# A graph network on one NeuronCore: the last scaling of the output moves from VectorE and ScalarE to GpSimd

## The reference, cut to what matters

```python
def _layernorm(x, axis=-1, eps=1e-5):
    m = jnp.mean(x, axis=axis, keepdims=True)
    v = jnp.var(x, axis=axis, keepdims=True)
    return (x - m) / jnp.sqrt(v + eps)

# layer 0: two gated steps (m = adj @ (x @ W), gates by sigmoid and tanh), each with a relu
x = _layernorm(x + _L0_gnn_ref(x, adj, ...))
# layer 1: each row weighs its last 100 neighbours by powers of 1/2
support = input @ weight
mask = (adj != 0)
rank = jnp.cumsum(mask, axis=1); deg = rank[:, -1:]
k = jnp.minimum(deg, 100.0); pos = rank - (deg - k)
w = mask * jnp.where(pos > 0, 0.5 ** (k - pos), 0.0)
x = _layernorm(x + w @ support + bias)          # this layernorm's division is what the change moves
```

## Time and profile before

| what | value |
|---|---|
| median of 3 executions | 377.87 us (377.56 to 378.74) |
| the profiled execution | 378.1 us, of it the span of the profile 376.4 us |
| TensorE busy | 350.5 us (93%) |
| VectorE busy | 301.3 us (80%) |
| ScalarE busy | 152.6 us (41%) |
| GpSimd busy | 25.6 us (7%), 16 powers of it 23.7 us |
| last stores | 8 of 128 KB, 1.9 us from issue to landing |

### The profile page before, as it was taken

The page is one execution under the profiler, slowest core; times in us unless marked ns, Lnnn a source line. Parts: engine busy times, 40 slices in busy tenths (PEclk is TensorE's granted clock), DMA queues, the critical chain, the costliest instruction groups (busy, mean ns, idle before and its releaser), DMA issues.

```text
span 376.4 us, 6453 instructions
## 1 busy us (share of the span) xinstructions
PE 350.5 (93%) x2424; PEld 161.3 (43%) x2424; DVE 301.3 (80%) x476; ACT 152.6 (41%) x185; POOL 25.6 (7%) x32
## 2 busy tenths in 40 slices
PE   4896979999999999999999889999999999979993
PEld 1331324243333333333332224353544453869992
DVE  1488979797876968889966597969897999888993
ACT  0003303022031210312113246848677868676992
POOL 1000000000000000000000020202020201102242
PEclk9999999999999999999999999999999999998999
DMA  7999999999999999998999999999999996100011
GB/s 231 404 393 392 409 381 407 376 410 362 407 405 351 386 300 407 376 367 341 343 348 321 398 377 352 341 339 336 356 346 369 379 374 237 30 0 4 2 57 57
DMA packets 36366, 117.38 MB, mean 312 GB/s; under 512 B 4208, under 2 KB 8560, under 8 KB 36336
## 3 DMA queue, kind: packets, MB, share of 16 engines
q1 hardware_dynamic: 36336, 116.97, 83.9%
HBM read 114.86 MB, written 1.05 MB: 308 GB/s over the span
## 4 chain that ended last, share of the span: by engine, by line
PE 71%; DMA 15%; ACT 5%; DVE 4%; issue 2%; POOL 1%; SPq 1%; POOLq 0%; DVEq 0%; ACTq 0%
PE m_acc L433 40%; DMA stream<-in_adj_t 12%; PE out L433 12%; PE out L533 6%; PE rz_ps L491 4%; PE n_ps L491 3%; PE rz_ps L506 3%; DMA hx<-in_x_pairs 2%; ACT codes L684 2%; PE m_acc L465 1%; ACT s_mid L684 1%; POOL rstd L775 1%; ACT stream L684 1%; PE out L475 1%; DVE codes L1015 1%
## 5 line engine op out<-in xcount | busy, mean ns | idle before, releaser
L433 PE MATMUL m_acc<-stream,s_in 128*64 128x512 f32 x512 | 126.7, 606 | 7.3 <-DMA stream<-in_adj_t 7.1
L834 DVE TENSOR_SCALAR codes<-stream 128x1024 uint8<-128x1024 f32 x128 | 83.8, 686 | 14.6 <-DMA stream<-in_adj_t 14.4
L433 PE MATMUL m_acc<-stream,s_mid 128*64 128x512 f32 x280 | 67.6, 604 | 1.7 <-DMA stream<-in_adj_t 1.7
L433 PEld LDWEIGHTS m_acc<-stream,s_in 128*64 128x64 f32 x512 | 34.0, 137 | 72.8 <-issue 44.6
L433 PE MATMUL out<-stream,s_mid 128*64 128x512 f32 x232 | 58.6, 594 | 0.3 <-DMA stream<-in_adj_t 0.2
L775 POOL TENSOR_TENSOR rstd<-var,mhalf 128x4 f32<-128x4 f32 x16 | 23.7, 1486 | 347.1 <-DVE var L983 347.1
L880 DVE SCALAR_TENSOR_TENSOR codes<-codes,run 128x1024 uint32<-128x1024 uint32 (+2 forms) x36 | 39.8, 1106 | 1.2
L875 DVE TENSOR_TENSOR run<-run,codes 128x2048 uint16<-128x2048 uint16 (+2 forms) x35 | 38.4, 1098 | 1.2
L684 ACT ACTIVATE wexp<-codes,code_bias 128x2048 uint16<-128x2048 uint8 x18 | 35.7, 1990 | 2.1 <-PE out L533 2.1
L684 ACT ACTIVATE codes<-codes,code_bias 128x2048 uint16<-128x2048 uint8 x16 | 31.6, 1987 | 0.0
L615 ACT ACTIVATE m_high<-m_acc 64x512 f32<-64x512 f32 x14 | 8.3, 594 | 57.2 <-PE m_acc L433 46.9
(11 more groups left out here) (143 smaller groups left out, 354.2 us busy)
## 6 DMA issues: line engine op xcount, KB each, us to landing
stream<-in_adj_t SPq DMA_DIRECT2D x212, 512.0 KB, 6.2
hx<-in_x_pairs SPq DMA_DIRECT2D x8, 128.0 KB, 8.4
mx<-in_x_t SPq DMA_DIRECT2D x8, 128.0 KB, 6.4
mx<-hx SPq DMA_DIRECT2D x16, 64.0 KB, 4.9
x_res<-in_x_pairs SPq DMA_DIRECT2D x8, 128.0 KB, 5.8
out_nodes<-stream SPq DMA_DIRECT2D x8, 128.0 KB, 1.9
const<-in_consts SPq DMA_DIRECT2D x1, 358.0 KB, 7.9
bias_b<-in_bias SPq DMA_DIRECT2D x1, 128.0 KB, 8.1
```

The source lines that it names most:

```text
L433: last = nc.tensor.matmul(to[D * u:D * (u + 1), :], state[:, t * D:(t + 1) * D], stream[:, n % SLOTS, u * CW:(u + 1) * CW], start=start[u] ...
L834: nc.vector.tensor_scalar(edges(p // 2, b, 2 * (p % 2), 2), stream[:, n % SLOTS, :], 0.0, None, ALU.not_equal).then_inc(mask_made, 1)
```

## The change

GpSimd scales all eight output chunks, each right behind its power, with one multiplication of 128x256 (`y` by `rstd`, both f32 in SBUF). It waits for its own power and for `y`. VectorE and ScalarE scale none: VectorE's loop loses five instructions and its tenth turn, ScalarE's loses twelve. SyncE waits for one semaphore instead of two.

```diff
-OUT_ACT = (0, 2, 4)
...
             for i in range(NCH):
-                if i in OUT_ACT:
-                    sp.wait_ge(o_by_act, OUT_ACT.index(i) + 1)
-                else:
-                    sp.wait_ge(o_by_dve, i + 1 - sum(a < i for a in OUT_ACT))
+                sp.wait_ge(out_scaled, i + 1)
                 sp.dma_start(out[NCH - 1 - i], o_n[:, i]).then_inc(out_stored, 16)
...
                 expand_next(ACT_END[i])
-                if i - 2 in OUT_ACT:
-                    b = i - 2
-                    act.wait_ge(rstd_made, NCH + b + 1)
-                    for k in range(KT):
-                        last = nc.scalar.activation(o_n[:, b, k, :], y[:, b, k, :],
-                                                    ACT.Copy, scale=rstd[:, b, k:k + 1])
-                    last.then_inc(o_by_act, 1)
...
             for i in range(NCH):
                 to_rstd(NCH + i, i)
+                pool.wait_ge(rstd_made, NCH + i + 1)
+                pool.wait_ge(y_made, i + 1)
+                nc.gpsimd.tensor_tensor(o_n[:, i], y[:, i],
+                                        rstd[:, i, :].unsqueeze(2).to_broadcast([P, KT, D]),
+                                        ALU.mult).then_inc(out_scaled, 1)
...
-            def scale_out(i):
-                dve.wait_ge(rstd_made, NCH + i + 1)
-                nc.vector.tensor_tensor(o_n[:, i], y[:, i],
-                                        rstd[:, i, :].unsqueeze(2).to_broadcast([P, KT, D]),
-                                        ALU.mult).then_inc(o_by_dve, 1)
...
-            for i in range(NCH + 2):
+            for i in range(NCH + 1):
...
-                if i >= 2 and i - 2 not in OUT_ACT:
-                    scale_out(i - 2)
```

More of the change, by code:

```diff
@@ L342, in build @@
         half_made, y_made = sem("half_made"), sem("y_made")
-        o_by_act, o_by_dve = sem("o_by_act"), sem("o_by_dve")
+        out_scaled = sem("out_scaled")
         out_stored = sem("out_stored")
```

## The result

| kernel | median | range | executions |
|---|---|---|---|
| before | 377.71 us | 376.77 to 384.1 | 20 |
| changed | 379.55 us | 377.74 to 518.4 | 20 |

A forecast was written before the change was run, and what follows sets the result against it. TensorE bounds the whole span; in the last 25 us TensorE, VectorE and ScalarE are in balance. The end's +1.16 and TensorE's +0.85 make +2.0 on the median of 377.87: 379.9 us, range 378.0 to 381.9.

The forecast's parts named there:

- X: Price of one 128x256 multiplication on GpSimd, taken as 0.65 us from the element-wise set-up instructions.
- rival B: A GpSimd multiplication costs 1.0 us or more, a power's fixed part being any TENSOR_TENSOR's; +1.1 unblocked, +4.1 blocked; chance 0.15.
- C: Rival: GpSimd pays some microsecond for each change between power and multiplication; over 381 us; chance 0.03.
- GpSimd's wait for its own instruction, 0.2: A GpSimd instruction that waits for the one before it starts 0.2 us behind its end.
- The end, +1.16: Behind TensorE's last share, two powers and two multiplications stand in one line on GpSimd; the end moves by +1.16 us.
- "Add eps" blocked: In the output loop "add eps" waits for the port that GpSimd's multiplication holds, 0.58 us late in each of four turns.
- TensorE's end, +0.85: Four slips of 0.58 less 0.68 for scalings gone delay chunk 6's `y` by 1.64; TensorE ends 0.85 us later.
- The sum, +2.0: The end's +1.16 plus TensorE's +0.85 us make the whole change +2.0 us slower.
- Rival A: "Add eps" needs no port or gets it first; TensorE ends 0.79 us earlier, +0.4 in all, 378.2 us; chance 0.31.

The follow-up runs named there:

- experiment 9: The changed kernel with chunk 6's multiplication in two pieces of 128x128 and chunk 7's in four of 128x64; one execution, 379.0 us.
- 1: The changed kernel, but GpSimd scales only chunks 0 to 5 and VectorE 6 and 7; ratio to the kernel before 1.0021, +0.8 us.
- 10: GpSimd scales chunks 0 to 5, VectorE 6 and 7, with "add eps" moved ahead of the expansion; ratio to the kernel before 0.9995, -0.2 us.
- 3: The changed kernel with "add eps" of the output chunks made a reduction over pairs; ratio to the kernel before 1.0008, +0.3 us.
- 6: The kernel before with only "add eps" of the output chunks made a reduction over pairs; ratio to the kernel before 0.9998, -0.1 us.
- 7: GpSimd scales chunks 0 to 5, each in two multiplications of 128x128, VectorE 6 and 7; ratio to the kernel before 0.9979, -0.8 us.
- 5: The kernel before with chunks 0 to 5 stored unscaled, VectorE scaling 6 and 7; ratio to the kernel before 0.9977, -0.9 us.
- 2: GpSimd scales only chunks 6 and 7, ScalarE and VectorE 0 to 5 as before; ratio to the kernel before 1.0033, +1.2 us.
- 4: GpSimd scales chunks 0 to 5, VectorE 6 and 7, with "add eps" of the output chunks a reduction; ratio to the kernel before 0.9971, -1.1 us.
- 8: "Add eps" a reduction, GpSimd scaling 0 to 6, VectorE 7, chunk 6's sum and "add eps" before the last-share wait; ratio to before 0.9977, -0.9 us.

## Why the prediction was right, and where its sizes were off

- **The multiplication, X = 0.65.** Measured 0.61. The guess from element-wise set-up instructions held, down to its parts: 0.19 fixed and 1.7 ns per element for two inputs, both as experiment 9 has them. The power's 1.01 is no fixed price of a TENSOR_TENSOR (one of 128x64 takes 0.29): rival B is out. So is C: a power behind a multiplication still takes 1.01.
- **GpSimd's wait for its own instruction, 0.2.** Measured 0.08 (373.06 to 373.14). Two of them make 0.24 of the error.
- **The end, +1.16.** Measured +0.79: 2 x 0.04 less for the multiplications, 0.24 less for the waits, 0.04 because the second power starts before the recorded end of the multiplication (373.71 against 373.75).
- **"Add eps" blocked.** The mechanism is shown: it holds in 1, 9 and 10, is absent where a reduction stands in the same place beside a running multiplication (3), and goes by half with half a multiplication (7). The size was 0.58 in the forecast and 0.43 in the trace. The prediction let GpSimd start 0.15 before VectorE's recorded end, but had VectorE wait for GpSimd's own recorded end. It doesn't: 0.59 from 356.29 ends at 356.88, less its normal 0.16 is 356.72, and the multiplication is recorded to 356.85. So VectorE gets the port 0.13 before GpSimd's recorded end, as GpSimd got it 0.13 before VectorE's here (356.85 - 0.61 = 356.24, the expansion is recorded to 356.37).
- **TensorE's end, +0.85.** With 0.43 the same sum gives 4 x 0.43 - 0.68 = +1.04 for `y` of chunk 6; the traces have 14.51 before (364.47 - 349.96) and 15.56 after (365.75 - 350.19) behind `y` of chunk 0. From `y` ready to the share: 368.71 - 366.22 = 2.49, forecast 2.47. Before, it was 368.20 - 364.94 = 3.26. So 1.05 - 0.77 = +0.28 is what was measured, instead of 0.85.
- **The sum, +2.0.** By these sizes it would have been +1.1. It was right in its sign and in each of its mechanisms, and 0.9 too high, by the terms "0.2" (GpSimd's wait for itself) and "0.58" (the slip) above all. The timed difference of +1.4 (0.8 to 2.0) contains the 0.4 outside the span, which no term stood for; without it, it is +1.0, next to the +1.1. So the closeness of 379.9 to the measured median of 379.55 is in part luck.
- **Rival A** (-0.79 at TensorE, +0.4 in all) is the case that 3 made true, with a stage 0.81 shorter. That 3 came out at +0.3 is a coincidence: by its trace it is -0.81 + 0.79 = 0.0, and 0.4 lies outside the span. The 0.79 itself is a figure of one execution: in the trace of 6, with the same stage of 18.23, TensorE waits 1.21 and 0.25 us for the two expansions and not 0.22 and 0.25, because it had come to the stage earlier.

The Trainium skill's "SBUF — State Buffer", section "Who interferes with whom", says that whoever of the two comes first has the shared pair and the other blocks. The trace agrees for the multiplication behind the expansion (1.55 instead of 0.61) and for "add eps" behind the multiplication (0.59 instead of 0.16). It doesn't agree for a power, as the last section shows.

## What to carry to other kernels

An engine that is nearly idle isn't free to use if it shares a port: look what stands behind the place where its instruction will be released, not how busy it is. Here 0.15 us of "add eps" turned harmless multiplications into a slip of 0.43 us per turn, and another form of the same small instruction gave it back. And work moved off a parallel engine at the very end of a kernel joins the chain there. Of the 0.79 us at the end of this kernel only about 0.2 is the slower engine (0.61 against 0.43 for the last multiplication); 0.6 is that the scaling of chunk 6, which had lain beside the last power on another engine, now stood in front of it.

## What the runs showed of the hardware that I had not expected

**A power seems to need the port at its start and at its end only.** In 3 a power (360.16, shown above) would have been done at 361.17. The expansion that began behind it at 360.56 ran its normal 1.22 to 361.78, and the power ended at 361.82. The expansion was not held up by a power that ran already, and the power waited until it was through. My reading is that the power had read its inputs, computed beside the expansion, and waited with its result. It is the same in every such pair: in 7 the power at 356.06 outlasts the expansion from 356.79 and ends 0.05 behind it. A scaling of VectorE with two SBUF inputs that started in the middle of a power (372.69) ran its normal 0.43. One that was under way when a power started held it up by 0.1 (1.11 instead of 1.01), which fits a read at the start.

**TensorE's clock after the same pause differs between executions.** In all twelve traces TensorE waits 2.6 us before its last node product. Windows of before around it, columns as in the earlier trace rows:

```profile
338.20:340.40 2.20, 2.20 (x8) 1.66 (x9) 2.20 (x2) 0.55 (x2) 0.00 (x0) 0.50 0.03 7
340.40:342.00 1.60, 1.60 (x25) 1.60 (x23) 1.25 (x4) 1.60 (x2) 0.57 (x1) 0.76 0.00 0
```

and of the changed kernel:

```profile
338.20:340.40 2.20, 1.57 (x15) 1.37 (x16) 2.17 (x4) 1.49 (x3) 0.00 (x0) 1.00 0.04 7
340.40:342.00 1.60, 1.60 (x33) 1.60 (x31) 1.57 (x4) 1.60 (x1) 0.34 (x1) 1.00 0.00 0
```

In the first the clock stood at the lower of its two levels, 1.2 GHz (0.50), for the whole first window behind the pause, and the four matmuls of that product took 2.08 us; in the other it stayed at 2.4 GHz and they took 1.13. There is a third kind, where the product began at the full clock and the clock fell later, while TensorE was busy. Windows of 5:

```profile
338.32:339.29 0.97, 0.97 (x5) 0.78 (x5) 0.97 (x1) 0.46 (x1) 0.00 (x0) 1.00 0.00 0
340.80:342.50 1.70, 1.70 (x18) 1.70 (x17) 1.37 (x3) 0.96 (x1) 1.35 (x1) 0.50 0.00 0
```

TensorE enters the last stage accordingly early or late against `y`. Its first share of chunk 6 (into `n_ps`) starts behind `y` of chunk 0 by 3.9 us where the clock stayed (changed, 1, 2, 4, 6), by 4.9 where it was low at once (before, 3, 9), and by 5.5 where it fell later (5, 7, 8, 10). The kinds occur with and without the change. Where ScalarE is the one that is late, this doesn't reach the end: the stage is 18.24 and 18.23 in 2 and 6 as in before, with 3.9 against 4.9, and 18.52 in 9 as in the changed kernel, with 4.9 against 3.9. Where ScalarE isn't late, it does: TensorE then needs 12.5 us from that first share to the share of `s_mid`, which makes 17.43 in 3 and 18.03 or 18.04 in 5, 7 and 8; only 4, with 3.9, comes down to 16.78, where ScalarE is again what it waits for. So the same relief of ScalarE was worth 1.5 us in one execution, 0.8 in another and 0.2 in a third. That this also makes the wide spread of these kernels' times is my reading and not tested.
